# One 48-row product for the last 16 items of every block, instead of three of 16 rows

## What is computed

```python
h = item_feat @ W_item.T + b_item                    # 10000 x 128
b = layernorm(x) @ W_user.T + b_user
x = x + relu(adj @ h + b)
...
# gate: idx = argmax(softmax(x_n @ gate_w + gate_b)); capacity C per expert
hmid = relu(einsum('ecd,edf->ecf', buf, w1) + b1)
ybuf = einsum('ecf,efd->ecd', hmid, w2) + b2
x = x + nan_to_num(ybuf[idx, pos] * prob * kept)
```

## Time and profile before

| | us |
|---|---|
| median of 3 runs | 1457.16 |
| lowest, highest | 1450.68, 1458.88 |
| the profiled execution, its own time | 1441.39 |
| its span, first to last instruction | 1439.6 |
| TensorE busy | 1365.8 (95%) |
| VectorE busy | 1167.7 (81%) |
| ScalarE busy | 983.8 (68%) |
| GpSimd busy | 565.1 (39%) |

### The profile page before, as it was taken

One profiled execution on the slowest core, in us unless ns is written; L12 is line 12 of the kernel. 1 busy time (PEld: TensorE's weight loads), 2 busy tenths in 40 slices (PEclk: granted clock), 3 DMA queues, 4 the chain that ended last, 5 costly groups with the idle time before them and its releaser, 6 DMA issues. The chain is left out here.

```text
span 1439.6 us, 20443 instructions
## 1 busy us (share of the span) xinstructions
PE 1365.8 (95%) x6318; PEld 1108.8 (77%) x6318; DVE 1167.7 (81%) x1714; ACT 983.8 (68%) x1010; POOL 565.1 (39%) x426
## 2 busy tenths in 40 slices
PE   7999999999999999999999999999999991899992
PEld 6878888888888888888888888888888871678771
DVE  7897978879879798798797987987979862388774
ACT  5686776767667767776677667766777650788870
POOL 0001235053151350532514405225144176288887
PEclk9999999999999999999999999999999995899996
DMA  8999999999999999999999999999999933323220
GB/s 331 354 416 409 362 361 352 355 354 353 360 352 355 353 353 355 353 357 354 359 351 353 355 352 358 350 362 345 362 352 362 347 118 101 91 76 93 72 67 3
DMA packets 88369, 434.31 MB, mean 302 GB/s; under 512 B 22526, under 2 KB 24070, under 8 KB 88328
## 3 DMA queue, kind: packets, MB, share of 16 engines
q1 hardware_dynamic: 67296, 416.42, 79.0%
q0 software_dynamic: 17952, 12.25, 3.2%
q10 hardware_dynamic: 3080, 5.12, 1.0%
HBM read 421.51 MB, written 23.50 MB: 309 GB/s over the span
## 5 line engine op out<-in xcount | busy, mean ns | idle before, releaser
L591 DVE TENSOR_TENSOR a_lo<-raw,a_hi 128x2000 fp32r<-128x2000 f32 (+1 forms) x400 | 863.3, 2188 | 145.1 <-ACT a_hi L427 141.3
L427 ACT CAST a_hi<-raw 128x2000 fp32r<-128x2000 f32 (+1 forms) x400 | 722.6, 1825 | 189.5 <-PE bank L939 164.3
L937 PE MATMUL bank<-a_hi,h_hi 128*128 128x500 f32 (+1 forms) x1580 | 636.1, 403 | 0.9 <-ACT a_hi L427 0.8
L939 PE MATMUL bank<-a_hi,h_lo 128*128 128x500 f32 (+1 forms) x1580 | 614.5, 389 | 0.0
L949 PE MATMUL bank<-a_lo,h_hi 128*128 128x500 f32 (+1 forms) x1580 | 428.5, 391 | 0.0
L937 PEld LDWEIGHTS bank<-a_hi,h_hi 128*128 128x128 f32 (+1 forms) x1580 | 297.4, 188 | 72.8 <-issue 17.9
L949 PEld LDWEIGHTS bank<-a_lo,h_hi 128*128 128x128 f32 (+1 forms) x1580 | 295.2, 188 | 71.8 <-issue 13.7
L939 PEld LDWEIGHTS bank<-a_hi,h_lo 128*128 128x128 f32 (+1 forms) x1580 | 298.3, 189 | 59.1 <-issue 4.4
L828 POOL TENSOR_TENSOR late<-ve,neghalf 125x4 f32<-125x4 f32 x20 | 22.4, 1121 | 666.4 <-DVE ve L608 666.4
L836 POOL DMA_INDIRECT records<-late,slot x80 | 194.3, 2429 | 22.9 <-issue 22.6
L902 POOL DMA_INDIRECT out<-raw,toki x128 | 134.4, 1050 | 35.7 <-issue 34.2
(11 more groups left out here) (114 smaller groups left out, 940.4 us busy)
## 6 DMA issues: line engine op xcount, KB each, us to landing
raw<-adj_m SPq DMA_DIRECT2D x380, 1000.0 KB, 5.3
raw<-adj_m SPq DMA_DIRECT2D x20, 500.0 KB
raw<-records SPq DMA_DIRECT2D x32, 202.1 KB
late<-items_t SPq DMA_DIRECT2D x19, 256.0 KB, 4.7
xb<-x ACTq DMA_DIRECT2D x20, 224.0 KB
raw<-w SPq DMA_DIRECT2D x8, 258.5 KB, 3.6
raw<-w SPq DMA_DIRECT2D x8, 256.0 KB, 2.9
out<-raw,toki POOLq DMA_INDIRECT x128
```

The costliest lines, as they stand in the source:

```text
L427: last = nc.scalar.copy(a_hi[:, g % HI_RING, 0:m], raw[:, g % RAW, 0:m])
L591: last = v.tensor_tensor(a_lo[:, g % RAW, 0:m], raw[:, g % RAW, 0:m], a_hi[:, g % HI_RING, 0:m].bitcast(F32), ALU.subtract)
L937: nc.tensor.matmul(acc[q][:, 0:BLOCK], h_hi[0:m, k * HID:(k + 1) * HID], a, start=(k == 0), stop=False)
L939: last = nc.tensor.matmul(acc[q][:, 0:BLOCK], h_lo[0:m, k * HID:(k + 1) * HID], a, start=False, stop=False)
```

## The change

The three products of the rest have 16 rows each. They become one product with 48 rows: partitions 0 to 15 hold hi(h) against hi(adj), 16 to 31 lo(h) against hi(adj), 32 to 47 hi(h) against lo(adj). The sum is the same.

For this the rest of `adj` lies three times over in memory and is loaded to 48 partitions; ScalarE casts all 48; VectorE writes its subtraction for partitions 32 to 47 over the cast there. `h_hi`'s columns of the rest get `h_lo` and `h_hi` in partitions 16 to 47, by two small transfers in SyncE's queue (`pack_h`), once, after block 1's load of group 2. TensorE waits for them (`h_packed`) in block 0. As the low part now reads slot 3 of `a_hi`, ScalarE's cast of group 3 waits, from block 1 on, for the low part of the previous block's group 19.

```diff
+PACK = 3 * REM
...
+                    if fixed and b == 1 and g == 2:
+                        pack_h()
                     if last:
                         rem_b = adj_r[b] if fixed else adj_r[bass.ds(b, 1), :, :].rearrange("o p n -> (o p) n")
-                        sp.dma_start(raw[0:REM, g % RAW, n:n + BLOCK], rem_b).then_inc(raw_loaded[g % RAW], 16)
+                        sp.dma_start(raw[0:PACK, g % RAW, n:n + BLOCK], rem_b).then_inc(raw_loaded[g % RAW], 16)
...
+            def pack_h():
+
+                sp.wait_ge(h_lo_ready, GROUPS)
+                cols = slice(FULL * HID, CHUNKS * HID)
+                sp.dma_start(h_hi[REM:2 * REM, cols].bitcast(F32), h_lo[0:REM, cols].bitcast(F32)).then_inc(h_packed, 16)
+                sp.dma_start(h_hi[2 * REM:PACK, cols].bitcast(F32), h_hi[0:REM, cols].bitcast(F32)).then_inc(h_packed, 16)
...
+                if g == HI_RING - 1 and (not isinstance(b, int) or b > 0):
+                    act.wait_ge(lo_used, b * GROUPS)
                 m, n = full_cols(g), group_cols(g)
                 last = nc.scalar.copy(a_hi[:, g % HI_RING, 0:m], raw[:, g % RAW, 0:m])
                 if m < n:
-                    last = nc.scalar.copy(a_hi[0:REM, g % HI_RING, m:n], raw[0:REM, g % RAW, m:n])
+                    last = nc.scalar.copy(a_hi[0:PACK, g % HI_RING, m:n], raw[0:PACK, g % RAW, m:n])
...
-                    last = v.tensor_tensor(a_lo[0:REM, g % RAW, m:n], raw[0:REM, g % RAW, m:n],
-                                           a_hi[0:REM, g % HI_RING, m:n].bitcast(F32), ALU.subtract)
+                    last = v.tensor_tensor(a_hi[2 * REM:PACK, g % HI_RING, m:n], raw[2 * REM:PACK, g % RAW, m:n],
+                                           a_hi[2 * REM:PACK, g % HI_RING, m:n].bitcast(F32), ALU.subtract)
...
             def low_part(b, q, g):
 
                 pe.wait_ge(lo_ready, b * GROUPS + g + 1)
-                for c in range(SIZES[g]):
-                    m = REM if FIRST[g] + c == FULL else 128
+                for c in range(min(SIZES[g], FULL - FIRST[g])):
                     k = FIRST[g] + c
-                    last = nc.tensor.matmul(acc[q][:, 0:BLOCK], h_hi[0:m, k * HID:(k + 1) * HID],
-                                            a_lo[0:m, g % RAW, c * BLOCK:(c + 1) * BLOCK],
-                                            start=False, stop=(k == CHUNKS - 1))
+                    last = nc.tensor.matmul(acc[q][:, 0:BLOCK], h_hi[:, k * HID:(k + 1) * HID],
+                                            a_lo[:, g % RAW, c * BLOCK:(c + 1) * BLOCK],
+                                            start=False, stop=False)
+                if g == GROUPS - 1:
+                    if isinstance(b, int) and b == 0:
+                        pe.wait_ge(h_packed, 32)
+                    c = FULL - FIRST[g]
+                    last = nc.tensor.matmul(acc[q][:, 0:BLOCK], h_hi[0:PACK, FULL * HID:CHUNKS * HID],
+                                            a_hi[0:PACK, g % HI_RING, c * BLOCK:(c + 1) * BLOCK],
+                                            start=False, stop=True)
...
-    adj_r = np.ascontiguousarray(adj_t[:, FULL * 128:]).reshape(BLOCKS, REM, BLOCK)
+    adj_r = np.tile(adj_t[:, FULL * 128:].reshape(BLOCKS, REM, BLOCK), (1, 3, 1))
```

More of the change, by code:

```diff
@@ L206, in build @@
         h_lo_ready = sem("h_lo_ready")
+        h_packed = sem("h_packed")
         raw_loaded = [sem(f"raw_loaded{i}") for i in range(RAW)]
@@ L932, in high_part @@
                 pe.wait_ge(hi_ready, b * GROUPS + g + 1)
-                for c in range(SIZES[g]):
-                    m = REM if FIRST[g] + c == FULL else 128
+                for c in range(min(SIZES[g], FULL - FIRST[g])):
                     k = FIRST[g] + c
-                    a = a_hi[0:m, g % HI_RING, c * BLOCK:(c + 1) * BLOCK]
-                    nc.tensor.matmul(acc[q][:, 0:BLOCK], h_hi[0:m, k * HID:(k + 1) * HID], a,
+                    a = a_hi[:, g % HI_RING, c * BLOCK:(c + 1) * BLOCK]
+                    nc.tensor.matmul(acc[q][:, 0:BLOCK], h_hi[:, k * HID:(k + 1) * HID], a,
                                      start=(k == 0), stop=False)
-                    last = nc.tensor.matmul(acc[q][:, 0:BLOCK], h_lo[0:m, k * HID:(k + 1) * HID], a,
+                    last = nc.tensor.matmul(acc[q][:, 0:BLOCK], h_lo[:, k * HID:(k + 1) * HID], a,
                                             start=False, stop=False)
```

## The result

Timed against the kernel before on one chip, six runs each, the changed kernel takes 1443.02 us (median; 1437.60 to 1446.47) where the kernel before takes 1452.16 (1450.68 to 1458.88). The ratio is 0.9924, with a 95% interval of 0.9899 to 0.9949: 7 to 15 us faster, about 11. The same two kernels on a second chip give 1428.95 against 1441.86 us, 0.9908 [0.9892 to 0.9925], or 12.9 us.

What follows compares the result with a forecast made beforehand. TensorE, busy 95% of the span, was taken as the bound. 19 x 0.855 = 16.2 us, less 0.5 for packing, gave 15.7 off the median of 1457.16, so 1441.5 us; range 1432 to 1452.

Steps and rivals of the forecast that it cites:

- The pair: Two 16-row products (hi x hi, lo x hi) in each block's high part; removing them saves 0.855 us of TensorE.
- 48 rows pay the change of height: The 48-row product on TensorE costs 0.615 us per visit, like the third 16-row product it replaces.
- the 16-row row: Trace rows of 16-row products between 128-row ones: 0.2 us per change of height, so 0.615 us for the 48-row visit.
- the 125-row row: Trace rows where 125-row transposes pass straight into 128-row products; the bound of no change cost, 0.225 us a visit.
- Rival 1: The 48-row product costs no change of height, 0.225 us a visit: 7.4 us more gained, 1434.1 us; chance 0.10.
- Rivals 2 to 4: Change times found again, 1449.1 us (chance 0.07); DMA bounds, 1460.7 us (0.08); ScalarE's new wait bounds, about 1493 us (0.05).
- the slack of 3.5 us: At each block's start, group 3's cast, 2.3 us later, still ends 3.5 us before TensorE asks for it.
- Packing, 0.5 us once: Block 1's two small copies delay SyncE's loads and TensorE's first 48-row product: 0 to 2 us once, 0.5 taken.
- The end: In the last block GpSimd, not TensorE, sets the end, so only that block's 0.855 us is lost.
- the chain behind 1195: The work after the last block's second GpSimd scaling, at 1194.97 us, keeps its length.
- the added wait: From block 1, ScalarE's cast of group 3 waits for the previous block's group 19 low part; cost 0.
- The doubt about the 16 us: Timed runs are 16 us slower than the profiled one, perhaps through something TensorE's work doesn't touch; would make the forecast wrong.

Runs made afterwards that it cites:

- own place: Changed kernel with the 48-row operand in unused columns of group 19's `a_lo` slot, so ScalarE's cast of group 3 needn't wait; 1426.35 us, 0.9891 of the kernel before.

## Why the prediction was right, and where a step of it failed

The forecast was 1441.5 us and 0.9892 of the median before; measured were 1443.02 and 0.9924 [0.9899, 0.9949]. That the time came so close is partly luck: two errors cancel. The gain was smaller than forecast (9 to 11 us, not 15.7), and the median of before, 1457.16 us from three runs, is 1452.16 with three more. On the second chip, without the stops, the gain is 12.9 us.

**The pair, 0.855 us per block: right.** The loop lost 0.84 per block, and the kernel before without the pair lost nearly the same (1103.0 to 1086.5 in 19 blocks, 0.87).

**48 rows pay the change of height: right.** 0.62 us for the visit against 0.615 forecast. The choice of the 16-row row over the 125-row row for the price was what mattered: 125 rows lie, by the run with 96, on the side where nothing is paid, 48 on the other. By the Trainium skill, "TensorEngine Tiling (Array Packing)", Key Properties and Tiling Modes, with When to Use Tiling, heights of up to 32 and up to 64 rows are tiling modes of their own and a switch drains the engine; the runs at 48 and 64 (paid) and 96 and 128 (not paid) agree with that border, at 0.39 us for a switch and back.

**Rival 1** was false for the kernel as it is, and its figure of 7.4 us was what filling the product up to 128 rows gives: 1087.0 less 1079.7 is 7.3 us in the loop, 7.8 in the measured time.

**Rivals 2 to 4: false.** The changes were not found again; DMA stayed no bound; TensorE never waited for the held-back cast, so the slack of 3.5 us that was worked out was not used up. (In that working the third 16-row product starts at 608.56, not near 608.67; nothing hangs on the 0.1 us.)

**Packing, 0.5 us once: nothing measurable.** TensorE does not wait for the copies: in block 0 the 48-row product starts 0.54 us behind the two full ones before it (86.25 to 86.79), as in the middle of the loop (599.68 to 600.22). SyncE's queue waits 9.3 us for `h_lo`, behind a backlog of loads that covers it.

**The end: this step failed.** I wrote that "the chain behind 1195 keeps its length", and it does; but I took the chain ahead of it, from 1155.87 to 1194.97, to move with the loop as a whole, and priced the added wait at 0 because TensorE does not feel it. VectorE does. In the last block the scaling starts 14.9 us ahead of the next users' product before (1170.8 less 1155.87), 14.4 with the shorter block alone (own place: 1154.6 less 1140.23) and 13.8 with the added wait (1154.9 less 1141.09; with the wait alone, in the kernel before, also 13.8). By then VectorE no longer pauses ahead of its two-input subtraction, so the subtraction begins first, the scaling that begins under it takes 2.94 us instead of 1.01, what follows slips too, and the first scatter comes 8.5 us ahead of that product instead of 11.7. The sum for the second chip is 16.0 (loop) less 3 = 13 us, against 12.9 measured; without the wait it is 15.5, where I had 15.7. The term of the sum that was mis-sized is the cost of the added wait with the end: 0 forecast, 3.0 us in the trace and 2.6 in the timed runs (1428.95 less 1426.35); added alone to the kernel before the wait costs 1.7 (0.9 to 3.5). It isn't a fixed price of the wait: with 128 rows the same 3.0 us are lost with the wait and without it. The end takes two lengths only. From the last users' product to the second scaling it is 24.2 us before, with the operand in its own place and with the pair left out, and 27.2 us in every other version, however early or late the first scaling starts in it.

**The doubt about the 16 us** between the timed runs and the profiled one was in place. The changed kernel's experts' stage is 21 us longer in the first comparison and 35 on the fourth chip than on the second, which shows none of these stops. No trace of the kernel before with such stops was taken, so that its slower timed runs are slow for this reason is argued, not shown. What the stops are is open. In the first profile of the changed kernel 11 of ScalarE's waits in that stage, 16.0 us in all, are put down to a remote semaphore, and the profile names nothing behind it; the same program on the second chip, and the kernel before, have no such wait at all:

```profile
ACT raw L553 <- remote: 16.0, 11, 3.6
```

The fastest version found is the one with 128 rows: 1421.13 us, 0.9858 [0.9842, 0.9875] of before on the second chip, and ahead of the changed kernel and of the kernel before on the fourth (1445.08 against 1452.37 and 1467.44).

## What to carry to other kernels

Where short contractions stand between full ones, count the changes of height as well as the products, and try filling the operand up with zeros before packing it tighter: here the extra rows were free and the change of height was not. A wait that the bounding engine never feels can still shift a third engine against a fourth, and tenths of a us decide which of the two begins first; look for the one place where the fourth sets the end, here the last pass of the loop. And compare a loop by a product that each pass has once, since the spans of two executions can differ by more than the change is worth.

## What the runs showed of the hardware that I had not expected

- What a GpSimd operation pays beside a VectorE subtraction with two inputs depends on which of the two begins first. Over all 14 traces the scalings of 125 x 4 elements that began 0.01 to 0.74 us ahead of a subtraction (24) took 1.01 to 1.02 us, though all ran on beside it for 0.27 us or more; those that began 0.04 to 0.25 us behind its start (284) took 2.89 to 3.08 us and ended 0.86 to 0.91 us behind its end, with next to no progress until it was through. A following operation of 125 x 1 took 4.11 us, begun under the first of two subtractions in a row. The Trainium skill, "GPSIMD Engine Reference", 1. Specifications, names SBUF interfaces shared by the two engines, with contention where a VectorE instruction has two inputs in SBUF; these rows agree where VectorE begins first, and give the size: up to the whole length of the instruction.
- A matrix product with more rows can be faster: 0.225 us for 128 rows against 0.62 for 48, between 128-row neighbours. 64 rows paid as 48 did, and 96 as little as 128.
- Of one program the same stage lasted 173.4 us on one chip and 208.2 on another, at an equal start.
